# An edge sum that multiplies each partial sum by the following weight, in place of a separate product stage

## The chip, the core and the metric

The kernel runs on one core of a Trainium2 chip. The core has TensorE (PE, matmuls into PSUM banks), VectorE (DVE), ScalarE (ACT), GpSimd (POOL, which here issues the gathers from HBM) and SyncE (SP, plain transfers). Each engine has its own program and works it off in order; engines wait for each other by semaphores. The metric is the device time of one execution in microseconds (us), lower is better, given as the median of several runs.

## The reference, cut to what matters

The whole program is a graph layer, an expert layer, a second graph layer and a small mixed MLP over 6250 nodes with 256 features. The change touches the second graph layer, which has two convolutions of this form:

```python
def _hconv(x, src, dst, ew, w1, b1, w2, b2, g, b):
    h = jax.nn.relu(x @ w1 + b1)
    msg = ew[:, None] * h[src]
    agg = jax.ops.segment_sum(msg, dst, num_segments=x.shape[0])
    h = agg @ w2 + b2
    return jax.nn.relu(_bn(h, g, b))
```

There are 100000 edges, sorted by destination. `dst` is 6250 times the square of a uniform number, so low node numbers have many edges and high ones few. `_bn` needs mean and variance of every column over all nodes.

## The kernel before

The program is a row of stages, each a block in which the five engines have their own instruction lists; a stage ends with a barrier. The part around the change is, twice: rows of messages are written to HBM (`h_rows`), `segment_sum`, `aggregate_product`, `norm_relu`.

**segment_sum.** The edges, padded to 784 tiles of 128, are worked off in 196 groups of G = 4 tiles. For one group:

- ACT copies the group's keys (L771) and its source indices as integers (L773, `idx`), which lets POOL go on.
- POOL issues four gathers of 128 rows of `h_rows` (L763) into one of RING = 7 slots of `msg`.
- ACT multiplies each landed row by its edge weight (L779) and tells PE (`scaled`).
- DVE builds the four 128x128 matrices of zeros and ones that say which edge goes to which node of a block of 128 nodes: L820 for the group's first block, L822 for a further one ("hot").
- PE multiplies messages by these matrices (L800, eight matmuls, 16 instruction records) into a PSUM bank: the sum of a block of nodes, transposed, so features lie on partitions. Banks 0 and 1 alternate for the first blocks, bank 2 is that of further blocks.
- DVE adds the bank to `c.T`, the 256 x 6250 result in SBUF (L828), and frees the group's slot.

Since edges are sorted, a group's edges fall into one block, or into two where a block ends (a further block; 48 of them, with 49 blocks). The block numbers come from a table that DVE and PE each read into registers (`node_tiles`, L749); a group with a further block runs a loop body in both programs. PE's order is: sums of group g, sums of its further block, sums of group g+1. DVE's order is: hot matrices of g+1, further block of g (matrices, add), add of g, table entry, hot matrices of g+2. The order is fixed in the code, in a loop of 28 passes over RING = 7 groups that ends with the last group's add. At the start DVE clears `c.T` (L839).

**aggregate_product.** For each of 25 column blocks of 256 nodes PE multiplies `c.T` by the weight (L924), ACT adds the bias and stores the product back to `c.T` (L910), DVE takes the statistics of the block (L934). At the end the statistics are combined (L942) to the scale and shift of the normalisation; ACT takes one root.

The helper `chain` makes an engine wait for its own instruction before it goes on; `take` waits for a semaphore and lowers it (L70 is the line of that wait).

Of the kernel before, what the change touches and what calls it, by code (L numbers as in the profile page):

```python
# [20 lines left out]
ALU = mybir.AluOpType  # L21
# [703 lines left out]
def segment_sum(nc, c, edges, take_from, add_to, ranges, next_slot, next_w):  # L725

    def run(block, sb, sem):
# [4 lines left out]
        acc = c.ps[0:3]  # L740
# [4 lines left out]
        v, zero = sem("v"), sem("zero")  # L745
# [22 lines left out]
        def _(act):  # L768
# [22 lines left out]
            for h in range(LEAD, RING):  # L791
                scale(NG // RING - 1, h)

        @block.tensor
        def _(pe):
            def products(h, s):
# [7 lines left out]
            with pe.Fori(0, NG // RING) as q:  # L804
                for h in range(RING):
                    take(pe, scaled[h])
                    products(h, h % 2)
                    lo, hi = node_tiles(mybir.EngineType.PE, q * RING + h)
                    with pe.If(lo + 1 < hi):
                        with pe.Fori(lo + 1, hi):  # L810
                            products(h, 2)

        @block.vector
        def _(dve):
# [15 lines left out]
            def finish(h, lo, hi):  # L830
# [8 lines left out]
            chain(dve, dve.memset(c.T[:], 0.0), zero)  # L839
            with dve.Fori(0, NG // RING) as q:  # L840
                last = None
                for h in range(RING):
                    take(dve, keys_ready[h])
                    matrices(h, None, h % 2)
                    if last:
                        finish(*last)
                    last = (h, *node_tiles(mybir.EngineType.DVE, q * RING + h))
                finish(*last)
# [219 lines left out]


def aggregate_product(nc, c, w, w_ready, bias, gamma, beta):  # L1070

    def run(block, sb, sem):
        stats, agg = sb("stats", [P, KD, NJ, 6]), sb("agg", [P, KD, 2])
        out = c.ps[2:4]
        v, go, done, kept, stored = (sem(n) for n in ("v", "go", "done", "kept", "stored"))
        prod, out_free = pair(sem, "prod"), pair(sem, "out_free")

        @block.scalar
        def _(act):
            def store(j, s):  # L1080
                take(act, prod[s])
                chain(act, store_cols(act, c, j, out[s], bias), kept)
                act.sem_inc(out_free[s], 1)
                act.sem_inc(stored, 1)

            blocks(act, store)
            root_affine(act, c, go, done)

        @block.tensor
        def _(pe):  # L1090
            def product(j, s):
                take(pe, out_free[s])
                product_cols(pe, w, cols_block(c, j), out[s]).then_inc(prod[s], 1)

            pe.wait_ge(*w_ready)
            blocks(pe, product)

        @block.vector
        def _(dve):
            stat = stats_blocks(dve, c, stats, stored)  # L1100
            for s in range(2):
                dve.sem_inc(out_free[s], 1)
            with dve.Fori(0, NJ - 1) as j:
                stat(j, BLK)
            chain(dve, stat(NJ - 1, LAST), v)
            finish_affine(dve, c, stats, agg, gamma, beta, go, done, v)
# [1377 lines left out]
```

## Time and profile before

| | us |
|---|---|
| median of 3 runs | 5399.52 |
| lowest and highest run | 5396.0, 5408.83 |
| the profiled execution | 5405.47 |
| its span | 5403.7 |
| first segment_sum, first gather to last add | about 1017 |
| aggregate_product behind it, to the start of norm_relu | about 55 |
| second segment_sum and its aggregate_product | about 1017 and 54 |

Of the span PE is busy 70%, POOL 57%, DVE 37%, ACT 36%. These shares are means over stages with different limits; the two segment_sum stages and the products behind them take some 40% of the span. Rows of the trace name source line, engine, operation, and what is written and read. An engine's idle time is shown in front of an instruction, with what ended it; "L70" there is a wait for a semaphore. PEclk is TensorE's granted clock as a share of 2.4 GHz; it has two levels, 1.2 and 2.4 GHz.

### The profile page before, as it was taken

How to read it: one execution, taken by the hardware profiler on the slowest of the kernel's cores; microseconds unless marked ns; L12 is line 12 of the kernel's file. 1: busy time of each engine (PE TensorE's matmuls, PEld its weight loads, DVE VectorE, ACT ScalarE, POOL GpSimd, SP SyncE). 2: the span in 40 equal slices, each digit the busy share in tenths (PEclk: the TensorE clock that was granted, in tenths of full speed). 3: DMA queues.
4: the chain of work that ended last, by engine and by line, in shares of the span. 5: the costliest groups of instructions: out<-in, count | busy, mean ns of one | idle time of the engine just before them, and what ended most of it. 6: DMA issues, size and time to landing. Idle time of an engine off the chain costs nothing. (4 is left out here: it accounts for less than half of the span.)

```text
span 5403.7 us, 82597 instructions
## 1 busy us (share of the span) xinstructions
PE 3775.3 (70%) x19299; PEld 3215.4 (60%) x19306; DVE 2017.6 (37%) x5468; ACT 1956.5 (36%) x4823; POOL 3105.3 (57%) x2684
## 2 busy tenths in 40 slices
PE   3666666666657499999766666766556666665789
PEld 2555555555545388888655565666455566665567
DVE  6444444455547511111222222223422222224555
ACT  3222333332334222222343333333633333334543
POOL 5888888888840033333257777775177777772110
PEclk8777888888888799999877778788777777788899
DMA  8777766776670666666433333332133333331000
GB/s 248 88 88 88 88 88 88 88 87 88 87 186 25 171 184 185 185 184 184 119 103 102 102 102 101 103 101 78 64 103 101 103 102 102 103 101 34 24 16 25
DMA packets 373213, 569.87 MB, mean 105 GB/s; under 512 B 68039, under 2 KB 297099, under 8 KB 371188
## 3 DMA queue, kind: packets, MB, share of 16 engines
q0 software_dynamic: 210224, 344.84, 33.5%
q1 hardware_dynamic: 161652, 206.40, 12.4%
q10 hardware_dynamic: 1232, 17.43, 0.8%
q8 instruction: 42, 0.69, 0.1%
q14 instruction: 63, 0.52, 0.0%
HBM read 398.97 MB, written 169.49 MB: 105 GB/s over the span
## 5 line engine op out<-in xcount | busy, mean ns | idle before, releaser
L763 POOL DMA_INDIRECT A<-h_rows,segment_sum_idx x1568 | 1540.3, 982 | 699.3 <-issue 527.0
L800 PE MATMUL bank<-A 128*128 128x128 f32 x7808 | 1286.5, 338 | 758.7 <-PEq L70 757.9
L800 PEld LDWEIGHTS bank<-A 128*128 128x128 f32 x7808 | 1220.9, 249 | 824.5 <-issue 824.0
L448 POOL DMA_INDIRECT node_sums<-T,scattered_sum_idx x760 | 1181.6, 1555 | 241.6 <-issue 219.8
L779 ACT ACTIVATE A<-A,segment_sum_edge 128x256 f32<-128x256 f32 x1568 | 668.0, 496 | 1178.6 <-DMA A<-h_rows,segment_sum_idx 1178.6
L550 PE MATMUL bank<-X,T 128*128 x1952 | 624.1, 477 | 99.5 <-PEq L70 96.3
L544 PE MATMUL bank<-T 128*128 128x128 f32 x1952 | 346.1, 333 | 399.2 <-PEq L70 399.2
L828 DVE TENSOR_TENSOR T<-T,bank 128x256 f32 x488 | 205.3, 421 | 1104.0 <-DVEq L70 1104.0
L550 PEld LDWEIGHTS bank<-X,T 128*128 128x128 f32 x1952 | 456.9, 246 | 196.1 <-issue 121.1
L544 PEld LDWEIGHTS bank<-T 128*128 128x128 f32 x1952 | 305.5, 236 | 415.1 <-issue 410.7
L1641 POOL DMA_INDIRECT x_rows<-A,expert_ffn_ring_out x104 | 164.4, 1581 | 500.7 <-DMA x_rows<-A,expert_ffn_ring_out 258.5
L605 DVE SCALAR_TENSOR_TENSOR T<-T,edges,not_after 128x128 f32<-128x128 int16 x784 | 224.4, 348 | 546.5 <-DVEq L70 509.4
L820 DVE TENSOR_TENSOR A<-iota,segment_sum_edge 128x512 f32<-128x512 f32 x392 | 272.1, 694 | 342.8 <-DVEq L70 339.2
L1676 ACT ACTIVATE T<-bank,A 128x256 f32<-128x256 f32 x416 | 195.7, 473 | 463.3 <-ACTq L70 463.2
L492 ACT CAST scattered_sum_idx<-scattered_sum_goal 128x4 int32<-128x4 f32 x196 | 37.9, 193 | 662.9 <-ACTq L70 662.9
L475 ACT ACTIVATE T<-bank,rstd 128x512 f32<-128x512 f32 x244 | 167.6, 687 | 292.4 <-ACTq L70 292.4
L616 DVE TENSOR_SCALAR T<-iota,edges 128x128 f32<-128x128 f32 x784 | 228.0, 388 | 23.1 <-issue 5.7
L495 ACT ACTIVATE T<-bank 128x512 f32<-128x512 f32 x392 | 212.7, 595 | 39.3 <-ACTq L70 38.9
L1692 PE MATMUL bank<-A,T 128*128 128x256 f32 x832 | 196.4, 389 | 19.0 <-PEq L70 19.0
L924 PE MATMUL bank<-T,w 128*128 (+1 forms) x800 | 190.5, 395 | 13.8 <-PEq L70 13.6
L1692 PE MATMUL bank<-A 128*128 128x256 f32 x832 | 192.9, 386 | 0.0
L1692 PEld LDWEIGHTS bank<-A,T 128*128 128x128 f32 x832 | 147.6, 191 | 63.8 <-issue 40.7
(328 smaller groups left out, 4267.4 us busy)
## 6 DMA issues: line engine op xcount, KB each, us to landing
T<-in_L_ffn_W SPq DMA_DIRECT2D x52, 1024.0 KB
A<-in_L_ffn_W SPq DMA_DIRECT2D x52, 1024.0 KB
T<-src_lanes SPq DMA_DIRECT2D x196, 128.0 KB, 3.3
A<-h_rows,segment_sum_idx POOLq DMA_INDIRECT x1568, 2.8
A<-node_sums SPq DMA_DIRECT2D x36, 512.0 KB, 6.4
node_sums<-A ACTq DMA_DIRECT2D x2, 6528.0 KB, 30.6
h_rows<-A SPq DMA_DIRECT2D x50, 256.0 KB, 2.1
node_sums<-T,scattered_sum_idx POOLq DMA_INDIRECT x784, 4.0
```

The source lines that it names most:

```text
L448: pool.indirect_dma_start(c.sum_dram[at % COPIES], bass.IndirectOffsetOnAxis(ap=idx[:, h % LR, j:j + 1], axis=0), msg[:, h % LR * G + j, : ...
L495: ins = act.activation(msg[:, r * G + q * 2:r * G + q * 2 + 2, :].rearrange("p j d -> p (j d)"), out[s][q][:], ACT.Copy)
L544: mm = pe.matmul(mix[s][:, j * P:(j + 1) * P], picks[s][:, j, :], same[h % LR][:, j, :], start=True, stop=True)
L550: mm = pe.matmul(out[s][j // 2][:, j % 2 * D:(j % 2 + 1) * D], coef[p][:, j * P:(j + 1) * P], tile_at(c.X, b), start=(first and j % 2 == 0 ...
L605: ins = dve.scalar_tensor_tensor(same[r][:, j, :], lane[:, j * P:(j + 1) * P], c.edges[:, SRC, bass.ds(g * G + j, 1)], c.not_after[:], ALU ...
L616: ins = ts(picks[s][:, j, :], c.iota[:], key(j), c.edges[:, WEIGHT, bass.ds(g * G + j, 1)], ALU.is_equal, ALU.mult)
L763: pool.indirect_dma_start(msg[:, h * G + j, :], None, c.h_dram, bass.IndirectOffsetOnAxis(ap=idx[:, h, j:j + 1], axis=0)).then_inc(landed[ ...
L779: ins = act.activation(m, m, ACT.Identity, scale=edge[:, h, WEIGHT, j:j + 1])
L800: mm = pe.matmul(acc[s][:, k * P:(k + 1) * P], msg[:, h * G + j, k * P:(k + 1) * P], hot[:, s, j, :], start=(j == 0), stop=(j == G - 1))
L820: ins = dve.tensor_tensor(hot[:, s], cols, keys, ALU.is_equal)
L828: chain(dve, dve.tensor_tensor(cols, cols, acc[s][:, 0:D].rearrange("p (k n) -> p k n", k=KD), ALU.add), v)
L1692: mm = pe.matmul(ph[k % 2][:, 0:TOK], w1[s][:, d, k * P:(k + 1) * P], xe[:, d, :], start=(d == 0), stop=(d == KD - 1))
```

## The change

aggregate_product goes. segment_sum gets the weight, its bias and the parameters of the normalisation, and since the product is linear, it multiplies each block's partial sum by the weight before it is added to `c.T`:

- **DVE at the start:** `c.T` is filled with the bias (two copies of 128x6400 in place of the clearing), the statistics of one block of it are taken and spread over all 49 entries.
- **PE:** behind the sums of group g come the four matmuls (of 128 columns) of the weight with the held sum of group g-1. A further block's sums are multiplied at once, before the next group's sums.
- **DVE:** the bank is copied to SBUF (`hold`); the product, a group later, is added to `c.T`, and then the statistics of that block's 128 columns are taken again (`stat`). For a further block hold, product, add and statistics follow each other at once, with PE in between.
- **The loop** is one of 14 passes over 14 groups, with both last adds at the end.
- **The end:** the last block's statistics, then what aggregate_product did at its end.

```diff
+            def product(s):
+                take(pe, held[s])
+                for m in range(KD):
+                    for k in range(KD):
+                        mm = pe.matmul(out[s][:, m * P:(m + 1) * P], w[:, k, m * P:(m + 1) * P], part[s][:, k, :],
+                                       start=(k == 0), stop=(k == KD - 1))
+                mm.then_inc(multiplied[s], 1)
+
+            pe.wait_ge(*w_ready)
+            with pe.Fori(0, NG // TURN) as q:
+                for g in range(TURN):
+                    take(pe, scaled[g % RING])
+                    sums(g % RING, g % 2)
+                    if g:
+                        product((g - 1) % 2)
+                    lo, hi = node_tiles(mybir.EngineType.PE, q * TURN + g)
                     with pe.If(lo + 1 < hi):
                         with pe.Fori(lo + 1, hi):
-                            products(h, 2)
+                            sums(g % RING, 2)
+                            product(2)
+                product((TURN - 1) % 2)
...
+            def hold(s):
+                take(dve, summed[s])
+                dve.tensor_copy(part[s][:].rearrange("p k n -> p (k n)"), acc[s][:, 0:D]).then_inc(held[s], 1)
+
+            def stat(b, n):
+                for m in range(KD):
+                    ins = dve.bn_stats(stats[:, m, bass.ds(b, 1), :].rearrange("p a s -> p (a s)"), c.T[:, m, bass.ds(b * P, n)])
+                return ins
+
             def add(b, s):
-                take(dve, summed[s])
+                take(dve, multiplied[s])
                 cols = c.T[:, :, bass.ds(b * P, P)]
-                chain(dve, dve.tensor_tensor(cols, cols, acc[s][:, 0:D].rearrange("p (k n) -> p k n", k=KD), ALU.add), v)
+                chain(dve, dve.tensor_tensor(cols, cols, out[s][:, 0:D].rearrange("p (k n) -> p k n", k=KD), ALU.add), v)
+                chain(dve, stat(b, P), v)
+
+            def close(g, lo, hi):
                 with dve.If(lo + 1 < hi):
                     with dve.Fori(lo + 1, hi) as b:
...
-                        matrices(h, skip, 2)
+                        matrices(g % RING, skip, 2)
+                        hold(2)
                         add(b, 2)
-                add(lo, h % 2)
-                dve.sem_inc(slots_free[h], 1)
+                hold(g % 2)
+                dve.sem_inc(slots_free[g % RING], 1)
+
+            for m in range(KD):
+                ins = dve.tensor_copy(c.T[:, m, :], bias[:, m:m + 1].to_broadcast([P, NB * P]))
+            chain(dve, ins, begun)
+            chain(dve, stat(0, P), begun)
+            for m in range(KD):
+                ins = dve.tensor_copy(stats[:, m, 1:FULL + 1, :], stats[:, m, 0:1, :].to_broadcast([P, FULL, 6]))
+            chain(dve, ins, begun)
+            with dve.Fori(0, NG // TURN) as q:
+                ends = []
+                for g in range(TURN):
+                    take(dve, keys_ready[g % RING])
+                    matrices(g % RING, None, g % 2)
+                    if g:
+                        close(g - 1, *ends[g - 1])
+                    if g > 1:
+                        add(ends[g - 2][0], g % 2)
+                    ends.append(node_tiles(mybir.EngineType.DVE, q * TURN + g))
+                close(TURN - 1, *ends[TURN - 1])
+                add(ends[TURN - 2][0], TURN % 2)
+                add(ends[TURN - 1][0], (TURN - 1) % 2)
+            chain(dve, stat(FULL, LAST), v)
+            finish_affine(dve, c, stats, agg, gamma, beta, go, done, v)
```

DVE's program before, from the hot matrices of a further block (L822) on; bank2 is the further block's sum, bank0 the group's own, and the rows without operands are register work and branches:

```order
L822 SCALAR_TENSOR_TENSOR A<-iota,first,segment_sum12837_edge 128x512
L828 ISA
L828 TENSOR_TENSOR T<-T,bank2 128x2x128
L832 REGISTER_ALU
L832 COMPARE_AND_BRANCH
L831 UNCONDITIONAL_BRANCH
L828 ISA
L828 TENSOR_TENSOR T<-T,bank0 128x2x128
```

The same place in the program of the change (`hold` is L839, the add L849, the statistics L843; banks 3 to 5 hold products). The add of bank4 behind it, with its statistics, is left out here:

```order
L834 SCALAR_TENSOR_TENSOR A<-iota,first,segment_sum12837_edge 128x512
L839 COPY segment_sum12837_part2<-bank2 128x256
L849 ISA
L849 TENSOR_TENSOR T<-T,bank5 128x2x128
L843 ISA
L843 BN_STATS segment_sum12837_stats<-T 128x6
L843 ISA
L843 BN_STATS segment_sum12837_stats<-T 128x6
L854 REGISTER_ALU
L854 COMPARE_AND_BRANCH
L853 UNCONDITIONAL_BRANCH
L839 COPY segment_sum12837_part0<-bank0 128x256
```

Between a further block's matrices and the group's own bank stood one add; now a copy, an add and two statistics stand there, and PE's product lies between the first two. PE's program before, from a group's table entry on:

```order
L749 TENSOR_LOAD dst_ranges
L809 REGISTER_ALU
L809 COMPARE_AND_BRANCH
L810 UNCONDITIONAL_BRANCH
L800 MATMUL bank2<-A 128x128 x8
L810 REGISTER_ALU
L810 COMPARE_AND_BRANCH
L809 UNCONDITIONAL_BRANCH
L800 MATMUL bank1<-A 128x128 x8
```

And PE's program of the change at that place:

```order
L747 TENSOR_LOAD dst_ranges
L819 REGISTER_ALU
L819 COMPARE_AND_BRANCH
L820 UNCONDITIONAL_BRANCH
L799 MATMUL bank2<-A 128x128 x8
L807 MATMUL bank5<-segment_sum12837_part2,w1 128x128 x4
L820 REGISTER_ALU
L820 COMPARE_AND_BRANCH
L819 UNCONDITIONAL_BRANCH
L799 MATMUL bank1<-A 128x128 x8
L807 MATMUL bank3<-segment_sum12837_part0,w1 128x128 x4
```

The further block's product (bank5) stands directly behind its sums and waits for DVE's copy; the group's own product (bank3) comes only after the next group's sums.

## Rows read from the trace of the kernel before

**Rows 1.** Groups by line: count, busy us, mean ns, idle us before.

```profile
L763 POOL DMA_INDIRECT A<-h_rows,segment_sum_idx x1568 | 1540.3, 982 | 699.3 <-issue 527.0 <-POOLq L70 171.8 <-ACT segment_sum_idx L773 0.6
L828 DVE TENSOR_TENSOR T<-T,bank 128x256 f32 x488 | 205.3, 421 | 1104.0 <-DVEq L70 1104.0
```

**Rows 2.** First segment_sum: busy us (count) of PE, weight loads, DVE, ACT, POOL; PEclk.

```profile
2740.00:3757.00 1017.00, 644.53 (x3904) 611.87 (x3904) 279.48 (x488) 389.09 (x1173) 771.05 (x784) 0.78 0.35 101
```

**Rows 3.** POOL's waits from 3600 to 3757: us in total, times, longest.

```profile
POOL A L763 <- issue: 28.6, 94, 0.3
POOL A L763 <- ACT segment_sum_idx L773: 0.3, 1, 0.3
```

**Rows 4.** Timeline, DVE and PE late in the second segment_sum: start, us, engine, line.

```profile
4862.17 0.69 DVE L820 TENSOR_TENSOR A<-iota,segment_sum_edge 128x512 f32<-128x512 f32 x1 [1.02 <-DVEq L70]
...
4862.78 0.75 DVE L822 SCALAR_TENSOR_TENSOR A<-iota,first,segment_sum_edge 128x512 f32<-128x512 f32 x1
...
4863.67 3.81 PE L800 MATMUL bank<-A 128*128 128x128 f32 x32 [0.69 <-PEq L70]
...
4865.93 0.42 DVE L828 TENSOR_TENSOR T<-T,bank 128x256 f32 x1 [2.41 <-DVEq L70]
4866.85 0.42 DVE L828 TENSOR_TENSOR T<-T,bank 128x256 f32 x1 [0.50 <-DVEq L70]
...
4868.31 0.69 DVE L820 TENSOR_TENSOR A<-iota,segment_sum_edge 128x512 f32<-128x512 f32 x1 [1.03 <-DVEq L70]
...
4868.92 0.41 DVE L828 TENSOR_TENSOR T<-T,bank 128x256 f32 x1
...
4869.38 2.02 PE L800 MATMUL bank<-A 128*128 128x128 f32 x16 [1.90 <-PEq L70]
...
4870.97 0.75 DVE L822 SCALAR_TENSOR_TENSOR A<-iota,first,segment_sum_edge 128x512 f32<-128x512 f32 x1
```

**Rows 5.** L822 (further blocks) by stretches of 14 groups: DVE busy (count), PEclk.

```profile
3255.00:3326.00 71.00, 2.24 (x3) 0.81 0.35 100
3326.00:3400.00 74.00, 3.73 (x5) 0.79 0.35 101
3400.00:3468.00 68.00, 3.04 (x4) 0.75 0.36 104
3468.00:3543.00 75.00, 4.48 (x6) 0.79 0.35 102
...
3690.00:3757.00 67.00, 4.54 (x6) 0.94 0.32 93
```

**Rows 6.** Timeline early in the stage: a slow burst of PE, a lengthened gather.

```profile
2769.37 3.45 PE L800 MATMUL bank<-A 128*128 128x128 f32 x16 [2.08 <-PEq L70]
...
2773.06 0.42 DVE L828 TENSOR_TENSOR T<-T,bank 128x256 f32 x1 [3.40 <-DVEq L70]
2773.42 0.95 POOL L763 DMA_INDIRECT A<-h_rows,segment_sum_idx  x1 [0.30 <-issue]
...
2774.51 0.69 DVE L820 TENSOR_TENSOR A<-iota,segment_sum_edge 128x512 f32<-128x512 f32 x1 [1.03 <-DVEq L70]
2774.67 1.36 POOL L763 DMA_INDIRECT A<-h_rows,segment_sum_idx  x1 [0.30 <-POOLq L70]
```

**Rows 7.** Timeline around the end of segment_sum and of aggregate_product.

```profile
3754.43 2.87 PE L800 MATMUL bank<-A 128*128 128x128 f32 x16 [3.66 <-PEq L70]
3757.54 0.42 DVE L828 TENSOR_TENSOR T<-T,bank 128x256 f32 x1 [6.11 <-DVEq L70]
...
3806.01 0.75 DVE L934 BATCH_NORM_STATS2 aggregate_product_stats<-T  x2 [0.97 <-DVEq L70]
...
3807.53 0.44 DVE L934 BATCH_NORM_STATS2 aggregate_product_stats<-T 128x6 f32<-128x106 f32 x2 [0.77 <-DVEq L70]
3808.12 1.81 DVE L942 BATCH_NORM_AGGREGATE aggregate_product_agg<-aggregate_product_stats 128x2 f32<-128x150 f32 x2
...
3811.03 0.16 DVE L946 TENSOR_TENSOR affine<-affine,pcol 128x2 f32<-128x2 f32 x1
3811.34 0.16 DVE L947 TENSOR_TENSOR affine<-aggregate_product_agg,affine 128x2 f32<-128x2 f32 x1
```

**Rows 8.** DVE groups: the clearing of c.T, and a copy from SBUF to SBUF.

```profile
L839 DVE MEMSET T<- 128x12800 f32 x2 | 21.4, 10725 | 32.3 <-issue 25.0 <-ACT segment_sum_idx L773 7.2
...
L267 DVE COPY A<-A 98x1024 f32<-98x1024 f32 x1 | 1.1, 1084 | 0.2 <-DVEq L70 0.2
```

More of the change, by code:

```diff
@@ L722, in root, with segment_sum @@
     act.sqrt(x[:], x[:]).then_inc(done, 1)
-def segment_sum(nc, c, edges, take_from, add_to, ranges, next_slot, next_w):
+def segment_sum(nc, c, edges, take_from, add_to, ranges, next_slot, next_w, w, w_ready, bias, gamma, beta):
+    TURN = 2 * RING
+    assert NG % TURN == 0
     def run(block, sb, sem):
@@ L739, in run @@
         idx, edge = sb("idx", [P, RING, G], I32), sb("edge", [P, RING, 3, G])
-        acc = c.ps[0:3]
+        acc, out = c.ps[0:3], c.ps[3:6]
+        part = [sb(f"part{s}", [P, KD, P]) for s in range(3)]
+        stats, agg = sb("stats", [P, KD, FULL + 1, 6]), sb("agg", [P, KD, 2])
         rings = lambda name: [sem(f"{name}{h}") for h in range(RING)]
@@ L744, in run @@
         hot_ready, summed = [sem(f"hot_ready{s}") for s in range(3)], [sem(f"summed{s}") for s in range(3)]
-        v, zero = sem("v"), sem("zero")
+        held, multiplied = [sem(f"held{s}") for s in range(3)], [sem(f"multiplied{s}") for s in range(3)]
+        v, begun, go, done = (sem(n) for n in ("v", "begun", "go", "done"))
         def node_tiles(eng, g):
@@ L792, in _, with sums @@
                 scale(NG // RING - 1, h)
+            root_affine(act, c, go, done)
         @block.tensor
         def _(pe):
-            def products(h, s):
+            def sums(h, s):
                 take(pe, hot_ready[s])
@@ L802, in products @@
                 mm.then_inc(summed[s], 1)
[L804 to L808, printed above, removed]
+            def product(s):
[13 more added lines that the diff above has]
+                    lo, hi = node_tiles(mybir.EngineType.PE, q * TURN + g)
                     with pe.If(lo + 1 < hi):
                         with pe.Fori(lo + 1, hi):
-                            products(h, 2)
+                            sums(g % RING, 2)
+                            product(2)
+                product((TURN - 1) % 2)
         @block.vector
@@ L833, in finish @@
                         skip = nc.s_assert_within(b - lo, 1, FULL, skip_runtime_bounds_check_because=CLAMPED)
-                        matrices(h, skip, 2)
+                        matrices(g % RING, skip, 2)
+                        hold(2)
                         add(b, 2)
-                add(lo, h % 2)
-                dve.sem_inc(slots_free[h], 1)
[L839 to L848, printed above, removed]
+                hold(g % 2)
[22 more added lines that the diff above has]
+            finish_affine(dve, c, stats, agg, gamma, beta, go, done, v)
     stage(nc, run, "segment_sum")
@@ L1067, in summed_product @@
     stage(nc, run, "summed_product")
[L1070 to L1106, printed above, removed]
-    stage(nc, run, "aggregate_product")
 def norm_product(nc, c, w, w_ready, bias, gamma, beta):
```

9 lines of the change are left out of this document (4 added, 5 removed).

## The prediction, made before the change was run

> **What bounds the kernel now.** I read first the groups by line for what a gather costs, then the busy time of the engines over one whole segment_sum, then POOL's waits, then the timeline of DVE and PE where further blocks are dense. A gather takes 982 ns in the mean [rows 1], and in front of each POOL idles 28.6 us / 94 = 0.304 us that nothing in the profile explains, while it waits for ACT's indices just once, 0.3 us [rows 3]. So POOL issues without pause: 1.286 us a gather, 5.14 us a group, 72.0 us for 14 groups. In the stage's 1017 us its 784 gathers fill 771 us; the rest is that fixed gap. PE is busy 645 us and DVE 279 us there [rows 2]. The gathers set the stage's length. But DVE's 279 us understate it: its program is a serial chain, and what it needs per group must be read from the timeline. aggregate_product behind it is not hidden by anything.
>
> **What the change takes away.** In the first stage the last add starts at 3757.54 and ends at 3757.96; the combining of the statistics starts at 3808.12 [rows 7]. Those 50.2 us go. What stands there instead, counted from the last group's sums: PE starts them at 3754.43, DVE reads the bank 3.11 us later [rows 7]. Then hold 0.42, hop to PE 0.14, product 1.36 (both below), by which time the add of the group before, with statistics, has just ended; add 0.42, chain 0.27, statistics 0.49, and the last block's statistics 0.25 + 0.44: some 7.4 us after the sums' start where the old add ended at 3.5. That gives 3.9 back. Combining 294 values a feature in place of 150 must cost more than 0.91 us each [rows 7]: between nothing and twice that, 1 us for the two. Saved per stage 50.2 - 3.9 - 1.0 = 45.3, in both **91 us**.
>
> **What DVE's chain needs before.** From [rows 4]. A group without a further block: matrices to add 0.61 (4868.31 to 4868.92), add 0.42, then 1.03 to the next matrices (wait for its own add, table entry, next keys): 2.06 us. A further block puts between: matrices, 0.89 to PE's start (4862.78 to 4863.67, of it 0.14 the hop), 2.26 until DVE's add starts (4865.93), and 0.92 to the next add: 4.07 us. The check: from one L822 to the next two groups later, 4862.78 to 4870.97, is 8.19 us, and 2 x 2.06 + 4.07 = 8.19. POOL needs 10.3 us for two groups, so this chain was never the bound, but it was near.
>
> **What the change adds to the chain.** A PSUM copy of 256 columns is costed as the add of that size, 0.42. Statistics: two of 256 columns take 0.75, two of 106 take 0.44 [rows 7], so two of 128 take 0.49. Between add and statistics stands a wait for its own add and one register step: at least 0.15, the gap between chained instructions (3811.03 + 0.16 to 3811.34), at most 0.50, the gap of four such steps [rows 7, 4]; I take 0.27, one step's worth above the low end.
> - A group: matrices 0.61, hold 0.38, add 0.42, chain 0.27, statistics 0.49, rest 0.96 (one semaphore step fewer than 1.03): **3.13 us**.
> - A further block: 0.89, sums until DVE reads them 2.16 (2.26 less one register step), hold 0.42 and hop 0.14, product, add with chain and statistics 1.18, 0.42 to the group's own hold. The product is eight records; the sums' sixteen at the quick level (2.02 a burst [rows 4]) make 0.111 us each, so 1.36 us until DVE's add in place of 2.26. Sum **6.57 us**. Nothing else can be done by DVE meanwhile, since hold and add wait for PE in the middle of its program, and behind them are queued the next groups' matrices, for which PE then waits.
> - The loop's end, once in 14 groups: nothing is prepared ahead of the last two closings, and after the jump DVE waits for the first sums: about 2.1 us.
>
> So 14 groups need 14 x 3.13 + 2.1 = 45.9 us plus 6.57 for each further block, against POOL's 72.0: the chain becomes the bound from **four further blocks in 14 groups** on. The counts in the last seven stretches are 3, 5, 4, 6, 6, 6, 6 [rows 5]; before them only one stretch has 4. With 5 the chain needs 78.8, with 4 72.2, with 6 85.3. Lateness at the end: 6.8 + 0.2 + 4 x 13.3 = 60 us a stage. The ring of seven slots only decides when POOL stops, not when DVE ends.
>
> **TensorE's level.** A burst of the sums took 2.02 us [rows 4] or, at the other level, 3.45 [rows 6]; in the late stretches the granted clock is 0.79 to 0.94 of 2.4 GHz [rows 5], a mix of both. At the slow level a further block costs 1.6 us more in its sums and 0.8 in its product, 9.0 in all. With a clock of 0.94 in the last stretch and 0.79 to 0.84 in those ahead, I estimate that one burst in six runs so in the chain; that share would add 0.4 to each further block: 74 us a stage. PE will be busier than before, which speaks for less; I take the middle, **67 us a stage, 134 in both**. The Trainium skill (TensorE: Matmul & The Clock Gate, Part 1) puts it that the default is the throttled clock and activity releases it; by that the upper end, 74, would not be reached.
>
> **What costs nothing.** PE's own work: 24 records of 0.111 us are 2.7 us a group at the quick level, below 5.14; at the slow one (3.45 for 16) they are 5.2, which would just fill its time. The start: two copies of 6400 at 1.06 ns (1084 ns for 1024 [rows 8]) make 13.6 us for the clearing's 10.7, plus under 3 us of statistics; the first sums come some 5 us later, and DVE has 26 us in hand in each of the first two loop passes. Its cover is that slack; without it, 10 us in both stages. The matrices lengthen a gather that they meet (1.36 against 0.95 us, beside an L820), an add that reads PSUM does not [rows 6]. Their number stays; I price the shift in phase at nothing, and bound it by none at all (982 in the mean against 0.95 us undisturbed: 25 us less a stage) and by 0.4 us for each in the first 100 groups (some 40 us more a stage, the present share taken off: 30). ACT keeps its work.
>
> The sum: -91 + 134 = **+43 us**. Against the profiled execution, 5405.5, that is 5448; it lies 6 us above the median, so the forecast is 5399.5 + 43 = **5442 us**.
>
> **Rivals.**
> 1. *The chain stays behind the gathers.* The steps overlap better than I read (a copy or statistics much shorter, hold early). At 2.9 and 6.1 us the lateness is 29 us a stage and the time 5367; at none, 5309. For it: DVE is busy only 27% of the stage. Against: the check of 8.19 us, where waits already filled the chain. Chance 0.18.
> 2. *The slow level holds in the chain.* PE waits for DVE between short bursts and keeps the slow clock: 9.0 us a further block, six in 14 groups need 100 us, lateness 152 a stage: 5399.5 - 91 + 304 = 5612. Decides if most further blocks' sums take 3.4 us. Against: late stretches have the highest clock now. Chance 0.07.
> 3. *About even.* Per group 3.05, per further block 6.3: 45 us a stage, 5399. Chance 0.17.
> 4. *POOL is held up too.* The opening copies from SBUF to SBUF block gathers for as long as they run, or matrices fall on gathers more often: at worst 2 x 14 + 2 x 30 us on top, 5530. No row shows such a copy beside a gather; in segment_sum only matrices lengthen one [rows 6]. The Trainium skill (SBUF — State Buffer, Who interferes with whom) says that an fp32 copy within SBUF can take the port that GpSimd writes descriptors through, and that an instruction with two SBUF inputs meets only GpSimd's reads; by it the copies would cost at most their own length, once a stage. Chance 0.10.
> 5. *The change does not do what it says.* The order of a further block ahead of the next sums was there before, so that part moves nothing; the product is new work in any case.
>
> **The numbers.** The forecast's own case, from 5416 to 5480, has 0.48. A measurement of this kernel can tell 0.3% (16 us) from no change. Faster by more than that: 0.18 (rival 1); within it: 0.17 (rival 3); slower: 0.48 + 0.07 + 0.10 = 0.65. The range leaves out rival 2 and the lower half of rival 1, 0.16 in all, and takes in the rest: 5365 to 5530.
>
> **What would show it.** In the changed profile: no 50 us stage behind the edge sums; the first half of each segment_sum at 72 us per 14 groups, the last four stretches near 85 to 88; POOL waiting there for indices where it never did; two L834 two groups apart 12.8 us from each other; DVE's read of bank 2 to its add of bank 5 about 1.9 us. If POOL shows no such waits, or the last stretches stay at 72, the chain was mis-sized and the time is near 5310. If sums in the late stretches take 3.4 us, rival 2 holds.

## The result, and the profile after

The changed kernel takes **5549.39 us** (four runs, 5545.59 to 5554.16) beside 5403.05 for the kernel before on the same chip: a ratio of **1.0268, 95% interval 1.0255 to 1.0281**. The direction was forecast, the size was not: +146 us against +43, and the time lies above the range. Spans of the profiled executions: 5548.2 and 5403.7, a difference of 144.5.

What was to go did go. The last add of the first segment_sum and what follows (start, us, engine, line):

```profile
3878.39 0.42 DVE L849 TENSOR_TENSOR T<-T,bank 128x256 f32 x1 [0.35 <-DVEq L70]
3879.05 0.49 DVE L843 BATCH_NORM_STATS2 segment_sum_stats<-T  x2 [0.24 <-DVEq L70]
3879.86 0.44 DVE L843 BATCH_NORM_STATS2 segment_sum_stats<-T 128x6 f32<-128x106 f32 x2 [0.32 <-DVEq L70]
3880.45 1.48 DVE L977 BATCH_NORM_AGGREGATE segment_sum_agg<-segment_sum_stats 128x2 f32<-128x294 f32 x1 [0.15 <-DVEq L70]
```

From the last add's end (3878.81) to the combining are 1.6 us where 50.2 stood [rows 7]: 48.6 less in this stage, and 47.4 less in the second. But the last add starts at 3878.4 where it started at 3757.5, and in the second stage at 5100.0 instead of 4915.6. Of those 184 us the first gather of that stage brings 74 along, so the two stages became **121 and 110 us longer** where 67 each was forecast. The account: -96 + 231, and some 10 us of small things (combining 1.48 us each in place of 0.91, and 6 us more behind it in the program's last part, whose cause stays open), is the 144.5.

Where a stage got longer is seen from stretches of 14 groups, cut at the first matrices of each loop pass. L834, the further blocks' matrices, with DVE busy (count), PEclk and DMA:

```profile
3342.15:3427.28 85.13, 3.73 (x5) 0.90 0.35 102
3427.28:3508.70 81.42, 2.98 (x4) 0.90 0.31 88
3508.70:3602.49 93.79, 4.48 (x6) 0.86 0.28 81
3602.49:3697.89 95.40, 4.47 (x6) 0.86 0.27 78
3697.89:3790.28 92.39, 4.47 (x6) 0.89 0.27 79
3790.28:3878.40 88.12, 4.46 (x6) 0.89 0.15 44
```

With 4, 5 and 6 further blocks the forecast was 72.2, 78.8 and 85.3 us; it is 81.4, 85.1 and 92 to 95, some 6 to 10 us more. The last stretch, also with six, is only 88.1: it stops at the last add, with no jump and no new start behind it. The chain of DVE and PE is the bound there, and the granted clock in the mean is not to blame: 0.86 to 0.90, where [rows 5] has 0.75 to 0.81 in the first four stretches and 0.94 in the last. POOL waits for indices, which it did once in that time before [rows 3] (3600 to 3757: us in total, times, longest):

```profile
POOL A L761 <- POOLq L70: 46.8, 16, 7.4
```

**The steady chain is as forecast.** Two groups with a further block in the first of them (DVE, with one row each of POOL and PE, second segment_sum):

```profile
4931.64 0.75 DVE L834 SCALAR_TENSOR_TENSOR A<-iota,first,segment_sum_edge 128x512 f32<-128x512 f32 x1
4931.80 1.41 POOL L761 DMA_INDIRECT A<-h_rows,segment_sum_idx  x1 [0.30 <-issue]
...
4934.71 0.42 DVE L839 COPY segment_sum_part<-bank 128x256 f32<-128x256 f32 x1 [2.33 <-DVEq L70]
4935.28 1.13 PE L807 MATMUL bank<-segment_sum_part,w 128*128 128x128 f32 x8 [0.73 <-PEq L70]
...
4936.67 0.42 DVE L849 TENSOR_TENSOR T<-T,bank 128x256 f32 x1 [1.54 <-DVEq L70]
4937.34 0.49 DVE L843 BATCH_NORM_STATS2 segment_sum_stats<-T  x2 [0.24 <-DVEq L70]
...
4940.69 0.69 DVE L832 TENSOR_TENSOR A<-iota,segment_sum_edge 128x512 f32<-128x512 f32 x1 [0.95 <-DVEq L70]
...
4943.72 0.76 DVE L832 TENSOR_TENSOR A<-iota,segment_sum_edge 128x512 f32<-128x512 f32 x1 [0.94 <-DVEq L70]
...
4944.40 0.74 DVE L834 SCALAR_TENSOR_TENSOR A<-iota,first,segment_sum_edge 128x512 f32<-128x512 f32 x1
```

L834 to L834 is 12.76 us (forecast 12.8); reading bank 2 to adding bank 5 is 1.96 (1.9); a group is 3.03 (3.13; the shortest of all is 3.01); so a further block is 12.76 less two groups of 3.02 to 3.03, 6.7 (6.57; by the shortest of the groups with one, 9.64, it is 6.63). Statistics 0.49 and the gap before them 0.24 were forecast as 0.49 and 0.27.

**The end of a pass is not.** Here the pass before group 154 ends (DVE, then PE):

```profile
3584.05 0.69 DVE L832 TENSOR_TENSOR A<-iota,segment_sum_edge 128x512 f32<-128x512 f32 x1 [0.93 <-DVEq L70]
...
3586.32 0.42 DVE L849 TENSOR_TENSOR T<-T,bank 128x256 f32 x1 [0.56 <-DVEq L70]
...
3588.65 0.75 DVE L834 SCALAR_TENSOR_TENSOR A<-iota,first,segment_sum_edge 128x512 f32<-128x512 f32 x1 [1.18 <-issue]
...
3595.60 0.42 DVE L849 TENSOR_TENSOR T<-T,bank 128x256 f32 x1
...
3598.12 0.42 DVE L849 TENSOR_TENSOR T<-T,bank 128x256 f32 x1 [1.38 <-DVEq L70]
3598.78 0.49 DVE L843 BATCH_NORM_STATS2 segment_sum_stats<-T  x2 [0.24 <-DVEq L70]
3602.49 0.69 DVE L832 TENSOR_TENSOR A<-iota,segment_sum_edge 128x512 f32<-128x512 f32 x1 [3.22 <-DVEq L70]
3603.35 0.69 DVE L832 TENSOR_TENSOR A<-iota,segment_sum_edge 128x512 f32<-128x512 f32 x1 [0.16 <-DVEq L70]
3607.23 0.42 DVE L839 COPY segment_sum_part<-bank 128x256 f32<-128x256 f32 x1 [3.19 <-DVEq L70]
3608.15 0.69 DVE L832 TENSOR_TENSOR A<-iota,segment_sum_edge 128x512 f32<-128x512 f32 x1 [0.49 <-DVEq L70]
```

```profile
3595.83 2.05 PE L807 MATMUL bank<-segment_sum_part,w 128*128 128x128 f32 x8 [2.40 <-PEq L70]
3603.33 6.37 PE L799 MATMUL bank<-A 128*128 128x128 f32 x32 [5.45 <-PEq L70]
```

From the last group's matrices (3584.05) to those of the third group of the next pass (3608.15) are 24.1 us. Three groups and the one L834 between need 3 x 3.02 + 6.63 = 15.69 in the steady chain, so this end costs **8.4 us**, where the forecast had 2.1. It has four pieces:

- The last group's further block starts its matrices 4.6 us behind the group's own, because the hold of the group before and the add of the one before that come first in the program; within the pass it starts 0.61 us behind.
- The last add stands alone, 2.52 us behind the one before it.
- In front of the next pass's first matrices DVE shows 3.22 us of idle time where a steady group has 0.93.
- PE, idle for 5.45 us, begins the new pass with a slow burst: from 3603.3 to 3607.0 the granted clock is 0.50, the level of 1.2 GHz, and DVE reads the bank 3.88 us behind the second matrices. The level had fallen before that idle time: the pass's last product took 2.05 us for 8 records, where the one at 4935.28, within a pass, took 1.13. All seven late passes of both stages begin so: 3.1 to 3.3 us from the first record of the burst to its sixteenth, where the quick burst at 4932.53 takes 1.7.

Counted like the 8.4 us, the ends of the seven late passes cost 7.3 us in the mean in the first stage and 7.4 in the second.

**The start is held up too.** The first rows of the changed stage:

```profile
2739.71 6.89 DVE L863 COPY T<-pcol 128x6400 f32<-128x6400 f32 x2 [22.34 <-PEq L98]
...
2741.19 5.54 POOL L761 DMA_INDIRECT A<-h_rows,segment_sum_idx  x1 [71.94 <-POOLq L70]
...
2747.03 0.98 POOL L761 DMA_INDIRECT A<-h_rows,segment_sum_idx  x1 [0.30 <-issue]
```

The first gather takes 5.54 us and ends 0.13 us behind the copies (2746.60). In the kernel before it took 1.08, with the clearing beside the next ones. The copies themselves are twice as fast as forecast: 6.89 us for both, not 13.6.

### The profile page after: what moved, and what is told of

Same layout as the page of the kernel before. It is cut to its first block and busy times, and to the rows that moved or that the text cites. A ratio compares the mean times of both kernels' runs of the same rounds, so it can differ in the third digit from the quotient of the medians.

```text
span 5548.2 us, 92225 instructions
## 1 busy us (share of the span) xinstructions
PE 4018.5 (72%) x22809; PEld 3450.7 (62%) x22810; DVE 2398.8 (43%) x6846; ACT 1921.9 (35%) x4723; POOL 3098.8 (56%) x2684
## 5 line engine op out<-in xcount | busy, mean ns | idle before, releaser
L799 PE MATMUL bank<-A 128*128 128x128 f32 x7808 | 1126.9, 307 | 507.0 <-PEq L70 505.3
L799 PEld LDWEIGHTS bank<-A 128*128 128x128 f32 x7808 | 1059.0, 219 | 560.7 <-issue 560.2
L807 PE MATMUL bank<-segment_sum_part,w 128*128 128x128 f32 x3904 | 555.4, 288 | 156.6 <-PEq L70 156.5
L807 PEld LDWEIGHTS bank<-segment_sum_part,w 128*128 128x128 f32 x3904 | 502.8, 202 | 189.0 <-issue 189.0
L839 DVE COPY segment_sum_part<-bank 128x256 f32<-128x256 f32 x488 | 206.1, 422 | 519.3 <-DVEq L70 513.8
L849 DVE TENSOR_TENSOR T<-T,bank 128x256 f32 x488 | 204.5, 419 | 233.7 <-DVEq L70 233.1
L769 ACT COPY segment_sum_edge<-edges 128x12 f32 (+1 forms) x392 | 75.1, 192 | 657.5 <-ACTq L70 650.5
L843 DVE BATCH_NORM_STATS2 segment_sum_stats<-T (+1 forms) x984 | 240.9, 285 | 129.9 <-DVEq L70 125.9
```

The costliest lines, as they stand in the source:

```text
L799: mm = pe.matmul(acc[s][:, k * P:(k + 1) * P], msg[:, h * G + j, k * P:(k + 1) * P], hot[:, s, j, :], start=(j == 0), stop=(j == G - 1))
L807: mm = pe.matmul(out[s][:, m * P:(m + 1) * P], w[:, k, m * P:(m + 1) * P], part[s][:, k, :], start=(k == 0), stop=(k == KD - 1))
L839: dve.tensor_copy(part[s][:].rearrange("p k n -> p (k n)"), acc[s][:, 0:D]).then_inc(held[s], 1)
L843: ins = dve.bn_stats(stats[:, m, bass.ds(b, 1), :].rearrange("p a s -> p (a s)"), c.T[:, m, bass.ds(b * P, n)])
```

## The experiments

**My theory after the two traces:** the steady chain is right, and the ends of the passes (with the jump back of a long loop body), some slow bursts and the start make the rest. The jump back is DVE's step from the last instruction of a loop pass to the first of the next. Rival A: the ends matter little, the chain is longer everywhere. Rival B: a longer loop body costs DVE time in itself, whatever the stage does.

### Passes of 7 and of 28 groups

```diff
-    TURN = 2 * RING
+    TURN = RING          (turn7)
+    TURN = 4 * RING      (turn28)
```

> The changed kernel with loop passes of 7 groups in place of 14 (28 passes a stage; DVE's loop body is half as long). Theory A, the end of a pass is dear by itself (both last sums, products and adds drain before anything new is prepared): twice as many ends, so about 5530 to 5570 us, although each jump back is short again (0.3 us). Theory B, the dear part is the jump back of DVE's long body, 3.0 us in the changed kernel where it was 0.32 before: that goes with the short body, and the time is 5480 to 5505.

> The changed kernel with loop passes of 28 groups (7 a stage). Theory A: half of the ends go; of the seven passes of 14 in which the chain is the bound some 3.5 ends of 12 us fall away a stage, 84 us in all, about 5465. Theory B: only half of the jumps go, 2.7 us each: 5530. If the number of passes does not matter at all (rival: the chain inside the pass is simply longer than read): 5549.

Measured beside 5403.46 for the kernel before: passes of 7 groups 5538.77 us (ratio 1.0247, 1.0229 to 1.0264), passes of 28 groups **5496.55** (1.0173, 1.0156 to 1.019). The kernel with passes of 7 (DVE at its 154th group):

```profile
3587.38 0.42 DVE L849 TENSOR_TENSOR T<-T,bank 128x256 f32 x1 [1.38 <-DVEq L70]
3588.04 0.49 DVE L843 BATCH_NORM_STATS2 segment_sum_stats<-T  x2 [0.24 <-DVEq L70]
3589.29 1.53 DVE L832 TENSOR_TENSOR A<-iota,segment_sum_edge 128x512 f32<-128x512 f32 x2 [0.76 <-DVEq L70]
```

and with passes of 28 (at its 168th):

```profile
3668.35 0.42 DVE L849 TENSOR_TENSOR T<-T,bank 128x256 f32 x1 [1.38 <-DVEq L70]
3669.01 0.49 DVE L843 BATCH_NORM_STATS2 segment_sum_stats<-T  x2 [0.24 <-DVEq L70]
3673.23 0.69 DVE L832 TENSOR_TENSOR A<-iota,segment_sum_edge 128x512 f32<-128x512 f32 x1 [3.73 <-DVEq L70]
```

The gap in front of the pass's first matrices is 0.76 us with the short body, 3.22 and 3.73 with the long ones. The rest of the end as far as shown is the same, the slow first burst too (13 of 14 late passes in either stage). Counted as above, an end in the late half costs (mean of the first stage, of the second):

| passes of | ends in the late half | us an end | together |
|---|---|---|---|
| 7 groups | 14 | 4.3, 4.6 | 60, 65 |
| 14 groups (the change) | 7 | 7.3, 7.4 | 51, 52 |
| 28 groups | 3 | 7.6, 7.1 | 23, 21 |

So the jump is about 2.7 us of an end and the drain of the chain 4.5. Passes of 7 save the one and pay the other twice, and gain almost nothing; passes of 28 halve both. They gain 53 us, 26 a stage, and the table gives 28 to 31 a stage for the late half. For 7 groups theory A's range held. For 28 the time lies between theory A (5465) and theory B (5530): I had taken all of the unexplained time for ends. Rival A falls, since the number of passes alone moves 53 us and the steady intervals stand as forecast.

### Is it the long body in itself?

The kernel before, with passes of 28 groups in place of 7:

```diff
+    TURN = 4 * RING
...
-            with dve.Fori(0, NG // RING) as q:
+            with dve.Fori(0, NG // TURN) as q:
```

> The kernel before with passes of 28 groups in place of 7, nothing else: DVE's loop body becomes as long as the changed kernel's. Expected: DVE's jump back takes about 3 us as in the changed kernel (if the length of the body is what makes it long) in place of 0.32, and the time stays within 5 us of before, 5403, since the gathers bound that kernel and DVE has slack. If the jump stays at 0.3, the long jump has another cause than the body's length.

Measured 5403.3 (ratio 1.0001, 0.9991 to 1.001). Here too the jump is long, 3.08 us in the median against 0.32 in the kernel before, and the queue that the page calls "instruction" moves more. The kernel before, the same with passes of 28, and the change:

```profile
q14 instruction: 63, 0.52, 0.0%
```

```profile
q14 instruction: 147, 1.20, 0.1%
```

```profile
q14 instruction: 210, 1.72, 0.1%
```

(packets, MB, share). With passes of 7 groups the changed kernel has 63 again. The longer body makes the jump long in either kernel, but in the kernel before the gathers cover it and the time does not move. So rival B is right about the jump and wrong about the time: only a chain at its limit pays for an end.

### The opening copies

```diff
-            for m in range(KD):
-                ins = dve.tensor_copy(c.T[:, m, :], bias[:, m:m + 1].to_broadcast([P, NB * P]))
-            chain(dve, ins, begun)
+            chain(dve, dve.memset(c.T[:], 0.0), begun)
```

> The changed kernel with the clearing of before (one memset of 128x12800) in place of the two bias copies; the bias is left out of the sum, which the normalisation behind it takes away again. Theory: the copies hold up the first gather by 4.6 us a stage (5.54 against 0.95), and since all later gathers follow it, 9 us come back: 5540. Rival: the hold-up is absorbed by slack: 5549.

Measured 5537.05 (1.0243, 1.0226 to 1.026), 12 us below the change. The two ratios differ by 0.0025, a little more than their intervals leave open. The first gather is free again:

```profile
2740.19 1.08 POOL L761 DMA_INDIRECT A<-h_rows,segment_sum_idx  x1 [72.59 <-POOLq L70]
...
2741.43 10.72 DVE L862 MEMSET T<- 128x12800 f32 x1 [25.02 <-issue]
2741.57 0.98 POOL L761 DMA_INDIRECT A<-h_rows,segment_sum_idx  x1 [0.30 <-POOLq L70]
```

The copies hold the first gather up by 4.5 us in each stage. What this costs in the end is less sure: counted from first gather to last add, the first stage is 9.4 us shorter without the copies, the second 1.2 us longer. So the total fits the 9 us that were expected, but the traces do not show them stage by stage. The Trainium skill (SBUF — State Buffer, Who interferes with whom) says that an fp32 copy within SBUF can take the port through which GpSimd writes descriptors; the 5.54 us agree, and the hold-up ends with the copies. It also reasons that an instruction with two SBUF inputs meets GpSimd's reads and does not hold its descriptors up. Here gathers beside such instructions take 1.36 to 1.41 us in place of 0.95 (4931.80 above, and [rows 6]), so they are not free of them; whether the descriptors or the reading of the indices takes longer, no row tells.

### Taking work out of the chain

Three variants, and a fourth that joins them with the cleared `c.T`, were to show whether the chain is all of the lateness. One takes the statistics once, behind the last add; those at the start of the stage go too:

```diff
                 chain(dve, dve.tensor_tensor(cols, cols, out[s][:, 0:D].rearrange("p (k n) -> p k n", k=KD), ALU.add), v)
-                chain(dve, stat(b, P), v)
...
-            chain(dve, stat(FULL, LAST), v)
+            with dve.Fori(0, NJ - 1) as j:
+                stat(j, BLK)
+            chain(dve, stat(NJ - 1, LAST), v)
```

> The changed kernel with the statistics taken out of each add and taken over the whole of c.T in 25 blocks at the end, as the stage before did. Theory (VectorE's serial chain sets the late part): each of 244 adds a stage is 0.76 us shorter in the chain (0.27 gap, 0.49 statistics); the last passes fall from 94 to 79 us, the lateness from 115 to about 30 us a stage, and 19 us are paid at the end: 5549 - 2 x (85 - 10) = about 5395 to 5410. Rival (the chain waits for TensorE and the statistics lie in that wait): nothing comes back in the passes and 19 us a stage are added: 5587.

One defers the add of a further block, so that its sums, hold and product have the next group's work between them. For this the adds of group g-2 move ahead of the closing of group g-1:

```diff
-                        with pe.Fori(lo + 1, hi):
-                            sums(g % RING, 2)
-                            product(2)
+                        sums(g % RING, 2)
...
+                with pe.If(lo + 1 < hi):
+                    product(2)
...
+            def add_both(lo, hi, s):
+                add(lo, s)
+                with dve.If(lo + 1 < hi):
+                    with dve.Fori(lo + 1, hi) as b:
+                        add(b, 2)
...
+                    if g > 1:
+                        add_both(*ends[g - 2], g % 2)
                     if g:
                         close(g - 1, *ends[g - 1])
-                    if g > 1:
-                        add(ends[g - 2][0], g % 2)
```

> The changed kernel with the product of a further block put off like the others: TensorE multiplies it behind the next group's sums, and VectorE adds it two groups later, so that it never waits between hold and add. Theory (serial chain): the wait of hop and product, 1.5 us of each further block's 6.6, goes; the last passes fall by 8 us each, lateness 115 to about 65 a stage: 5437 to 5460. Rival (the order does not matter, TensorE's own work or the pass ends bound it): 5549.

One has both:

> Both of these at once. Theory: 14 groups with six further blocks need about 71 us, just what the gathers need; the lateness is gone and what is left is the old stage's 48.6 us less 19 for the statistics at the end, a stage, and some 5 a stage for the held-up first gather: about 5355. If the two savings do not add (another bound stands right behind, TensorE or the pass ends): above 5400.

and one has the deferral, the cleared `c.T` (the bias is left out) and each block's statistics once, when the groups move on:

> The deferred product, c.T cleared by a memset with the bias left out (the normalisation takes it away), and the statistics of a block taken once, when the next block of nodes is begun, in place of after every add. Theory: the gathers bound the whole of both edge sums and nothing is paid at the end: 5403 - 2 x 47 + a few us = about 5310 to 5325.

When these four were measured, the kernel before itself took **5983.73 us** instead of 5403, on another chip. They ran again on others, three of them beside the changed kernel, with these expectations:

> The statistics are taken once behind the last add instead of behind every add (one pair, 0.49 us and 0.24 us of gap, less for each group and each further block, some 0.73 x 490 = 360 us of VectorE work in both stages), and the end of the stage gets them back in 13 larger ones. If VectorE's chain sets the rate of the late stretches: 5395 to 5440 us. If what is late is the end of a pass (the jump back and TensorE's slow restart) alone, little is gained: 5530 us.

> The last further block of a group is held, and its product taken, behind the next group's sums, so that an iteration with further blocks has one round trip between TensorE and VectorE less; the statistics stay in the loop, the passes stay 14 groups long. My theory (the chain of the two engines in the stretches with many further blocks and at the end of a pass is what runs late): 5437 to 5460 us. Rival (the chain is not what sets the rate there; the gathers' descriptors are): 5549 us, as the change itself.

> The two edits together: the last further block deferred behind the next group's sums, and the statistics once at the end. Theory: the chain then falls below the gathers' 72 us for 14 groups in all but the last stretches: 5355 to 5400 us, as fast as the kernel before or faster. Rival (a pass's end and the clock stay): over 5420 us.

> As the deferral, and with T set to zero in place of the bias (the bias is left out of the result) and the statistics of a block taken once, when the groups move on to the next block, so nothing of them is left for the stage's end. Theory: the first gather is not held up (4.6 us a stage), and the statistics cost neither the steady chain nor the end: 5310 to 5345 us. Rival: not below the kernel before, over 5390 us.

> The changed kernel, as the measure for the three variants beside it. If the chip is like the one of its first runs: 5549 us, 1.027 of the kernel before. If it is like the two chips of the last runs, on which the kernel before takes 5984 to 6000 us: theory (the chain is longer where TensorE's ends come late, and every variant shortens it) 6480 to 6560 us, above each of the variants; rival (the variants take nothing out of the chain) 6420 us, as they are.

> The statistics once behind the last add instead of a pair behind every add. Theory: 5395 to 5440 us beside 5549 (on a slow chip 6418 to 6422 again, below the changed kernel). Rival (VectorE's work in the loop is hidden, and the end of a pass is what is late): 5530 us, within 0.4% of the changed kernel.

> The last further block of a group is held, and its product taken, behind the next group's sums. Theory: 5437 to 5460 us beside 5549 for the changed kernel (on a chip as slow as the last two, 6407 to 6419 us again, which is below the changed kernel). Rival (the round trips of the further blocks are not what is late): as the changed kernel.

> Both edits. If the chain is all of the lateness: 5355 to 5400 us, at or below the kernel before. If something else is late as well (the start, the slow restart of TensorE at the end of a pass): 5400 to 5450 us. On a slow chip 6483 us again.

> The deferral of the last further block and the statistics once at the end. On a chip like the first one: 5355 to 5400 us if the chain is all of the lateness, 5400 to 5450 us if the start and the slow restarts of TensorE are late as well. On a chip like the last three: 6440 to 6485 us again, 1.08 to 1.09 of the kernel before.

Each time the kernel before was as slow as that. Ratios to the kernel before as measured beside it (the second and the last row are the same chip):

| before, us | the change | statistics at the end | deferral | both | once |
|---|---|---|---|---|---|
| 5983.73 | | 1.0723 | 1.0705 | 1.0835 | 1.0738 |
| 5999.75 | | 1.0699 | 1.0702 | 1.0813 | 1.0714 |
| 5925.34 | 1.0882 | 1.072 | 1.0737 | 1.087 | |
| 5926.49 | | | | 1.0874 | |

The intervals reach 0.0018 to 0.0039 to either side. So on these chips each edit alone takes 96 to 98 us off the changed kernel (6452.75; 6354.52 and 6356.81), and the two together only 14 (6438.74). The changed kernel itself came out below the 6480 to 6560 us expected of it, but above both single edits, so the rivals that said "as the change itself" fall for these. That the chain is all of the lateness is not shown. That the two savings add was wrong, and the fourth variant, which was to be the fastest, is no better than the deferral alone. The times expected for a chip like the first were never tested.

A likely reason why both together fail can be read. The kernel with both, in plain groups (DVE):

```profile
3304.12 0.42 DVE L841 COPY segment_sum_part<-bank 128x256 f32<-128x256 f32 x1 [0.71 <-DVEq L70]
3305.03 0.69 DVE L834 TENSOR_TENSOR A<-iota,segment_sum_edge 128x512 f32<-128x512 f32 x1 [0.49 <-DVEq L70]
3306.98 0.42 DVE L851 TENSOR_TENSOR T<-T,bank 128x256 f32 x1 [1.26 <-DVEq L70]
3308.11 0.42 DVE L841 COPY segment_sum_part<-bank 128x256 f32<-128x256 f32 x1 [0.71 <-DVEq L70]
3309.02 0.69 DVE L834 TENSOR_TENSOR A<-iota,segment_sum_edge 128x512 f32<-128x512 f32 x1 [0.48 <-issue]
```

(here L834 are the first matrices, L841 the hold, L851 the add.) With the statistics at the end alone, such a group looks like this:

```profile
3113.65 0.69 DVE L832 TENSOR_TENSOR A<-iota,segment_sum_edge 128x512 f32<-128x512 f32 x1 [0.94 <-DVEq L70]
3114.26 0.42 DVE L839 COPY segment_sum_part<-bank 128x256 f32<-128x256 f32 x1
3114.59 0.41 DVE L849 TENSOR_TENSOR T<-T,bank 128x256 f32 x1
3115.93 0.69 DVE L832 TENSOR_TENSOR A<-iota,segment_sum_edge 128x512 f32<-128x512 f32 x1 [0.93 <-DVEq L70]
```

There hold and add follow the matrices without a wait, 2.28 us a group. The deferral puts the add ahead of the hold, so only one group's matrices stand between the hold of a sum and the add of its product, and each add waits 1.26 us: 3.99 us a group. A group with a further block goes the other way. The tenth percentile of each, from the four kernels of the table's third row, over both stages without the ends of passes (the short intervals, which TensorE's late ends, below, touch least):

| us | plain group | with one further block |
|---|---|---|
| the change | 3.03 | 10.32 |
| statistics at the end | 2.29 | 8.21 |
| deferral | 3.84 | 7.91 |
| both | 3.99 | 6.30 |

With 196 groups a stage and 48 further blocks, "both" pays 1.70 x 148 = 252 us and gets back 1.91 x 48 = 92 against the statistics at the end alone. That is 160 us a stage where 42 were measured; most of it, as an argument, lies in stretches that wait for gathers. The same reckoning makes the deferral alone about even with the change (0.81 x 148 = 120 against 2.41 x 48 = 116), and it is 48 us a stage faster. So it gives the direction and not the size, and it was not tried on its own. What the variants would take on a chip like the first stays unmeasured, and no version here beats the kernel before.

### What the slower chips do

> The kernel before, unchanged, for its trace. On a chip like the first one: 5403 us and last adds at 3757 and 4915 us. On a chip like the last three: 5925 to 6000 us; theory (TensorE itself comes late there, in every kernel): the last adds 250 to 290 us later a stage, and waits of VectorE of 5 us and more for sums whose matrices were long there; rival (the gathers are slower there): the mean of one gather above 982 ns.

Measured 5929.76. The last adds stand at 4016.4 and 5442.0 us: the first stage is 264 us longer than on the first chip (its last add comes 259 us later and its first gather 5 us earlier), the second 269 us. The gathers are not slower, 971 ns in the mean against 982 [rows 1]:

```profile
L763 POOL DMA_INDIRECT A<-h_rows,segment_sum_idx x1568 | 1522.2, 971 | 1235.8 <-issue 668.1 <-POOLq L70 551.9 <-ACT segment_sum_idx L773 15.7
```

DVE waits for sums that PE's records show as finished (the kernel before on the slower chip):

```profile
3315.78 2.02 PE L800 MATMUL bank<-A 128*128 128x128 f32 x16 [1.03 <-issue]
...
3324.16 0.42 DVE L828 TENSOR_TENSOR T<-T,bank 128x256 f32 x1 [8.53 <-DVEq L70]
```

The burst ends at 3317.8, its add starts 6.4 us later; on the first chip that takes 0.24 us (3757.30 to 3757.54, [rows 7]). In 107 of the 488 adds of this trace DVE sat idle over 2 us behind PE's last finished record, at most 13.6 us; in the trace of the first chip none did, at most 1.33. So TensorE, or its signal, comes late there, and the cause stays open. It is not shown either that it lies in the chip: no chip was met in both conditions, all slow measurements came after the quick ones, and the one chip met twice gave 5999.75 and then 5926.49 us. It does not touch the stages in which the expert layer runs: 1200 us of them have the same instruction counts to within ten on either chip. Everything said on the +146 us rests on the quick measurements; of the slow ones I use only comparisons with each other and the shortest intervals.

## Why the prediction was wrong in size

- **What is saved:** forecast 45.3 a stage; measured 48.6 and 47.4 between last add and combining, less 0.6 us for each of the two combinings of a stage; the 3.9 us for the end of the chain are in the lateness. Right. (The terms listed for the chain's end make 6.9 us and not 7.4, so 3.4; and one late stretch in [rows 5] has a clock of 0.75, below the 0.79 given. Neither moves the result.)
- **The steady chain:** 3.13 and 6.57 us forecast, 3.02 and 6.63 measured; 12.8 and 12.76 from L834 to L834. Right, and with it rival 1 (the chain hides) and rival 3 (about even) are out.
- **The step that failed is the loop's end:** "nothing is prepared ahead of the last two closings, and after the jump DVE waits for the first sums: about 2.1 us". It is 7.3 us in the late passes, 8.4 in the one shown. I had priced one wait for the first sums at the quick level. I left out the jump back of a body of 14 groups (2.7 us by the comparison with passes of 7), the last add that stands alone for its product, the last further block queued behind a hold and an add, and the slow level at which TensorE starts every late pass. Seven late passes at 5.2 us more are 36 us a stage, three quarters of the 48.5 that were missing in the mean of the two stages.
- **TensorE's level:** forecast 7 us a stage over the quick level. Outside the ends, the groups 112 to 195 of the change show 26 and 19 us beyond 3.02 and 6.63 a group and block, in slow bursts and short waits for rows. That is 12 to 19 more than forecast. Rival 2 (the slow level holds) is refuted within a pass: the median group with a further block takes 9.78 us, 6.8 more than a plain one, and not 9.0 more. At the start of a pass the slow level does hold.
- **The start "costs nothing": wrong.** Its slack of 26 us a pass was DVE's, but what was held up was POOL's first gather, which sets when all later ones start: 4.5 us in each stage, 12 us of the whole time in the run without the copies. Rival 4 named this mechanism, with 14 us a stage as its worst case.
- **The late stretches:** "near 85 to 88" was forecast for six further blocks; three of the four take 92 to 95, and the last, with no new start behind it, 88. That the ends make the difference is borne out by the steady intervals, which hold, and by the passes of 28.
- Added up for the late half of a stage: 67 forecast, + 36 for the ends, + 12 to 19 for bursts and waits, and - 7 because a steady group is 3.02 us and not 3.13, make 108 to 115; measured, from the first gather on, are 108 and 101. The other 12 and 9 us are there when the late half begins, where the forecast had none. The held-up gather can be up to 5 of them: without the copies they are 6 and 8. The rest stays open.

## What to carry to other kernels

A chain of two engines that is "never the bound" has to be priced at its seams as well as in its steady part: where a loop pass ends, the pipeline between the engines drains and fills, TensorE starts again at its slow level, and a jump back over a long body takes its time. All of that costs nothing until the chain is the bound. When moving a product into a producer's loop, ask which stretch is the densest, and compare its chain with the producer's rate; a mean utilisation of 27% said nothing here. An edit that removes a wait in the rare case can add one to every common case (by the short intervals 2.41 us less and 0.81 more here), so read both intervals.

## What the runs showed of the hardware

- VectorE's jump back takes 0.32 us for a loop body of 7 groups and 3.0 for 14 or 28 (medians 0.32, 0.33; 2.99, 3.07, 3.08), in both kernels, together with more packets on an instruction queue (63 with 7 groups; 210 in the change, 147 in the kernel before with 28).
- Two copies of 128x6400 elements within SBUF took 6.89 us together, half of what the copy in [rows 8] gives by its elements, and held a gather for 5.54 us; a clearing of the same area takes 10.72 us and holds none.
- Every late pass of the change begins with a burst of TensorE at its slow level (3.1 to 3.3 us for sixteen records in place of 1.7; granted clock 0.50 from 3603.3 to 3607.0). With passes of 28 it is the same, with passes of 7 in 13 of 14.
- The kernel before took 5403 us in the first measurements and 5925 to 6000 us, 9.7 to 11% longer, on three others. In the one slow trace of the kernel before, all of it lies in the two stages with edge sums, where DVE waits up to 13.6 us for sums that TensorE's records show as finished.
